# An edge loop on three engines: VectorE starts each tile at GpSimd's signal, one operand and three project steps moved

## The reference, cut to what matters

```python
def gatv2(x, src, dst, Ws, bs, Wd, bd, attn):
    H, D = attn.shape
    fs = (x @ Ws + bs).reshape(-1, H, D)
    fd = (x @ Wd + bd).reshape(-1, H, D)
    e = jax.nn.leaky_relu(fs[src] + fd[dst], 0.2)        # 10625 edges, gathered rows
    logits = jnp.einsum('ehd,hd->eh', e, attn)
    m = jax.ops.segment_max(logits, dst, num_segments=N)
    ex = jnp.exp(logits - m[dst])
    denom = jax.ops.segment_sum(ex, dst, num_segments=N)
    alpha = ex / denom[dst]
    out = jax.ops.segment_sum(alpha[:, :, None] * fs[src], dst, num_segments=N)
    return jax.nn.elu(out)

h = gatv2(x, src, dst, W1s, ...); h = layer_norm(h + x, ...)
out = layer_norm(gatv2(h, src, dst, Wos, ...), ...)      # the second graph attention
mix = mixer(xn)                                          # 12 heads, random features, then @ proj_w.T
x = x + out + mix; x = x + ffn(layer_norm(x))
```

## Time and profile before

| | |
|---|---|
| median of three runs | 1391.21 us (1389.6 to 1395.74) |
| the profiled execution | 1399.78 us, of it 1398.0 us span |
| loop 1, first lap's gather to last scatter | 105.56 to 434.26 us |
| loop 2, first lap's gather to last scatter | 652.52 to 999.53 us |
| busy share: PE, DVE, ACT, POOL | 76%, 66%, 40%, 44% |

### The profile page before, as it was taken

The page is one execution under the profiler, slowest core; times in us unless marked ns, Lnnn a source line. Parts: engine busy times, 40 slices in busy tenths (PEclk is TensorE's granted clock), DMA queues, the critical chain, the costliest instruction groups (busy, mean ns, idle before and its releaser), DMA issues.

```text
span 1398.0 us, 15907 instructions
## 1 busy us (share of the span) xinstructions
PE 1057.6 (76%) x5539; PEld 872.6 (62%) x5539; DVE 927.5 (66%) x1650; ACT 563.9 (40%) x736; POOL 616.7 (44%) x581
## 2 busy tenths in 40 slices
PE   5975655555542687898999999819587998999982
PEld 5963433333321687897787877617455997888871
DVE  6648777777774798544544454475358665999993
ACT  3304333333331898200434334420045324777760
POOL 1027777777773000014777777787400000333330
PEclk9988567778785789898799999958887899999995
DMA  9956666666766750257777776758423027999986
GB/s 335 354 193 174 197 199 196 195 198 196 203 197 169 174 163 1 79 144 232 227 218 220 198 214 191 257 161 246 103 77 118 6 102 279 396 399 406 399 329 176
DMA packets 85032, 290.84 MB, mean 208 GB/s; under 512 B 15970, under 2 KB 37768, under 8 KB 84341
## 3 DMA queue, kind: packets, MB, share of 16 engines
q0 software_dynamic: 34656, 145.11, 34.8%
q1 hardware_dynamic: 46822, 130.71, 27.7%
q10 hardware_dynamic: 3488, 14.16, 2.6%
HBM read 258.31 MB, written 31.62 MB: 207 GB/s over the span
## 4 chain that ended last, share of the span: by engine, by line
PE 37%; POOL 31%; issue 11%; DMA 9%; DVE 8%; ACT 3%; SPq 1%; DVEq 0%; POOLq 0%; ACTq 0%
POOL dense_logits L584 12%; PE ps L1461 10%; PE ps L1462 10%; PE ps L1463 10%; POOL ring_s L573 10%; POOL ring_d L579 9%; DMA ring_d<-table_dst,dst_i 4%; PE ps L1558 3%; PE ps L1542 1%; PE ps L1492 1%; DMA dl_b<-dense_logits 1%; DMA y_in<-y_rows 1%; DVE ring_s L1016 1%; DMA dl_a<-dense_logits 1%; ACT de L726 1%
## 5 line engine op out<-in xcount | busy, mean ns | idle before, releaser
L1016 DVE TENSOR_TENSOR ring_s<-ring_s,ring_d 128x776 f32<-128x776 f32 (+1 forms) x168 | 162.1, 965 | 244.1 <-DMA ring_d<-table_dst,dst_i 243.9
L573 POOL DMA_INDIRECT ring_s<-table_src,src_i x168 | 168.3, 1002 | 317.6 <-DVE fd_stage L945 257.8
L1521 PE MATMUL ps<-hot_s,hot_d 128*125 128x512 f16 (+1 forms) x840 | 185.5, 387 | 154.6 <-DVE hot_s L1023 154.5
L1521 PEld LDWEIGHTS ps<-hot_s,hot_d 128*125 128x125 f16 x840 | 116.1, 179 | 224.2 <-DVE hot_s L1023 165.0
L584 POOL DMA_INDIRECT dense_logits<-logits,cell_i x168 | 209.7, 1248 | 53.9 <-issue 50.0
L579 POOL DMA_INDIRECT ring_d<-table_dst,dst_i x168 | 168.9, 1005 | 76.7 <-issue 50.6
L700 ACT ACTIVATE hot_d<-iota_h,dst_bias 128x626 f16<-128x626 f16 x84 | 68.6, 816 | 217.5 <-PE ps L1521 217.5
L1461 PE MATMUL ps<-wp,at 128*125 128x384 f32 x300 | 107.3, 358 | 11.4 <-issue 4.4
L612 POOL COPY gather_i<-lst 128x1 int32 (+1 forms) x16 | 7.4, 462 | 237.7 <-DVE lst L1381 142.4
L1462 PE MATMUL ps<-wp,at 128*125 128x384 f32 x300 | 105.0, 350 | 0.0
L1463 PE MATMUL ps<-wp,at 128*125 128x384 f32 x300 | 104.8, 350 | 0.0
(11 more groups left out here) (252 smaller groups left out, 2338.9 us busy)
## 6 DMA issues: line engine op xcount, KB each, us to landing
eraw<-in_moe_w_dram SPq DMA_DIRECT2D x50, 768.0 KB, 6.7
raw<-in_moe_w_dram SPq DMA_DIRECT2D x44, 768.0 KB, 7.2
dense_logits<-neg ACTq DMA_DIRECT2D x1, 12288.0 KB, 43.6
mix_w<-in_qkv_wT_dram SPq DMA_DIRECT2D x18, 384.0 KB, 5.6
dl_a<-dense_logits SPq DMA_DIRECT2D x2, 2187.5 KB
dl_b<-dense_logits SPq DMA_DIRECT2D x2, 2187.5 KB
y_in<-y_rows SPq DMA_DIRECT2D x5, 672.0 KB
ring_s<-table_src,src_i POOLq DMA_INDIRECT x168, 4.1
```

The source lines that it names most:

```text
L573: pool.indirect_dma_start(out=ring_s[:, j, 0:WL[l]], out_offset=None, in_=table_src[l], in_offset=bass.IndirectOffsetOnAxis(ap=src_i[:, t: ...
L1016: dve.tensor_tensor(ring_s[:, j, 0:WL[l]], ring_s[:, j, 0:WL[l]], ring_d[:, j, 0:WL[l]], ALU.add).then_inc(z_ready[l], 1)
L1521: last = pe.matmul(ps[0:P, b, o:o + s1 - s0], hot_d[:, j, c * P:(c + 1) * P], hot_s[:, j, s0:s1], start=start and (n <= 5 or n == 9), stop ...
```

## The change

There are four edits.

1. **A signal and a wait.** Each lap of GpSimd that issues gathers raises `edge_turn[l]` by one, after its wait for `edge_done` and before the source gather (`pool.sem_inc`). In the program this makes one semaphore instruction a lap: it takes over the wait for `edge_done`, which was part of the gather's own instruction before. VectorE waits at tile t, for t from 3 to 81, until the signal of lap t - 3 has been given (`turn`).
2. **`total` moves to the front of a tile**, right behind the wait and ahead of `edge_sum`, in both loops.
3. **The attention row of loop 2 goes to PSUM.** `scale_attention(1)` writes it to `att_ps` in banks 6 and 7, and `weigh` reads it there. So the mixer may use six banks: `num` goes to bank 4 or 5 beside `kv`, at column `NUM_AT` = 130, and the transposes of the mixer's output use one pair of banks (4 and 5) instead of two, so that those of tile t wait for the low part of tile t - 1.
4. **`PROJ_FROM` becomes 67.** The last three project steps (17 to 19) then stand behind the last `total`.

```diff
-PROJ_FROM = ET - PROJ_STEPS
+PROJ_FROM = ET - PROJ_STEPS + 3
+TURN_LAG = 3
...
+        att_ps = ps[:, 6:8, :].rearrange("p a b -> p (a b)")[:, 1024 - D:1024]
...
-                b = (0 if n == 3 else 4) + 2 * (t % 2)
+                b = 2 * (t % 2) if n == 3 else 4
...
                     pool.wait_ge(edge_done[l], t + 1)
                     if t + G < ET:
+                        pool.sem_inc(edge_turn[l], 1)
                         gather_src(t + G)
                         gather_dst(t + G)
...
-                    last = act.copy(mix_out[:, :, 2 * r + h, :], ps[0:P, b, 0:T * (MD + 1)].rearrange(...))
+                    last = act.copy(mix_out[:, :, 2 * r + h, :], ps[0:P, b, NUM_AT:NUM_AT + T * (MD + 1)].rearrange(...))
...
-                dve.tensor_scalar(rows[:, 2, :], rows[:, 2, :], 0.8, None, ALU.mult).then_inc(att_scaled, 1)
+                dve.tensor_scalar((rows[:, 2, :], att_ps)[l], rows[:, 2, :], 0.8, None, ALU.mult).then_inc(att_scaled, 1)
+
+            def turn(l, t):
+
+                if TURN_LAG <= t < ET - G + TURN_LAG:
+                    dve.wait_ge(edge_turn[l], t - TURN_LAG + 1)
...
                 for t in range(ET):
+                    turn(0, t)
+                    if t >= 1:
+                        total(t - 1)
                     edge_sum(0, t)
                     if t + 1 < ET:
                         hot(t + 1)
                     weigh(t)
-                    if t >= 1:
-                        total(t - 1)
                     heads(t)
                 total(ET - 1)
...
-                    dve.scalar_tensor_tensor(out=ring_d[:, j, 0:D], in0=ring_s[:, j, 0:D], scalar=0.0, in1=rows[:, 2, :],
+                    dve.scalar_tensor_tensor(out=ring_d[:, j, 0:D], in0=ring_s[:, j, 0:D], scalar=0.0, in1=att_ps,
...
                 for t in range(ET):
-                    edge_sum(1, t)
+                    turn(1, t)
                     if t >= 1:
                         total(t - 1)
+                    edge_sum(1, t)
                     weigh(t)
...
-                back = (4, 1, 2, 2)[n]
+                back = (4, 1, 1, 2)[n]
...
+NUM_AT = 2 * (MD + 1)
...
-    if kind == "kv":
+    if kind in ("kv", "num"):
         return 4 + h
-    if kind == "num":
-        return 6 + h
```

More of the change, by code:

```diff
@@ L251, in build @@
         edge_done = [sem(f"edge_done{l}") for l in range(2)]
+        edge_turn = [sem(f"edge_turn{l}") for l in range(2)]
         scattered = [sem(f"scattered{w}") for w in range(W)]
@@ L813, in _ @@
                 else:
-                    last = act.copy(mix_out[:, :, 2 * r + h, :], ps[0:P, b, 0:T * (MD + 1)].rearrange("p (t d) -> p t d", t=T))
+                    last = act.copy(mix_out[:, :, 2 * r + h, :], ps[0:P, b, NUM_AT:NUM_AT + T * (MD + 1)].rearrange("p (t d) -> p t d", t=T))
                 last.then_inc(mix_used, 1)
@@ L1627, in _ @@
                         for f in range(2):
-                            last = pe.matmul(ps[0:P, b, t * (MD + 1):(t + 1) * (MD + 1)], mix_qp[:, h, f, t * P:(t + 1) * P],
+                            last = pe.matmul(ps[0:P, b, NUM_AT + t * (MD + 1):NUM_AT + (t + 1) * (MD + 1)], mix_qp[:, h, f, t * P:(t + 1) * P],
                                              mix_kv[:, h, f, :], start=f == 0, stop=f == 1)
```

## The result

| | before | after |
|---|---|---|
| median, same chip | 1397.37 us | 1389.61 us (1383.61 to 1396.2, 10 runs) |
| ratio | | 0.9957, 95% interval 0.9938 to 0.9976 |
| span of the profiled execution | 1398.0 us | 1388.3 us |

The change gains 6 us (3 to 9). I had forecast 32, and a time of 1359 us. The direction was right; the main step of the forecast was wrong. Single profiled executions lie several microseconds off their kernel's median, so times of steps read from profiles compare two kernels only that closely.

What follows compares the result with a forecast made beforehand. GpSimd's descriptor work was taken to bound loop 1, and loop 2 up to tile 64. Gains of 15 us (loop 1) and 17 us (end of loop 2) made 32, so 1391.2 - 32 = 1359 us; 8-in-10 range 1347 to 1400.

Steps and rivals of the forecast that it cites:

- the signal is given at least 0.76 us before the source gather starts: Loop 1: the running scatter covers the semaphore instruction's cost, and VectorE is held until near the scatter's start; 15 us gained.
- rival A: Both edge loops: the signal comes too early to hold VectorE, loop 1 gains 0, time 1379 us; chance 0.16.
- The arithmetic of the collision: GpSimd's jobs in the edge loops: one starting inside `edge_sum` is lengthened by the rest of `edge_sum` less 0.13 us.
- The free lap of 3.80 us: Edge loops: a GpSimd lap with nothing in its way takes 0.98, 0.97 and 0.94 us of work and three times 0.30.
- the 22 us: Loop 1: excess of scatter and gathers over their free durations, the most the edit can bring; 15 us of it taken.
- Rival B's locked case: Edge loops: `edge_sum` starts just before a GpSimd job every lap; with 0.6 us locked, 1435 us; rival's chance 0.22.
- whoever is first wins: Edge loops: VectorE's two-SBUF-operand instructions and GpSimd's descriptor work exclude each other at its start, the earlier one prevailing.
- Step 0 was to run at 904.4: Loop 2, first project step: reached at 901 with laps of 3.85 us, held by the mixer, 4.9 us earlier than before.
- 36 us for eight laps: Loop 2, step 0 to step 8's end: 35.1 plus a 3.8 us lap, less some 3 for `weigh` collisions; end at 940.5.
- Edit 4's overlap: End of loop 2: last `total` follows step 16's product, 14.5 us ahead of the last; dense stage begins 17 us earlier.
- Rival C: End of loop 2: logits loads go slower beside other traffic, that gain fails, 1370 us; chance 0.62 together with the main forecast.
- The mixer's end: Loop 2: the mixer runs at its own pace on TensorE and ScalarE, ends at 904.10 us; six banks cost nothing.

Runs made afterwards that it cites:

- e1: The changed kernel without the signal and without VectorE's wait for it: 1388.86 us, 0.9958 of the kernel before.
- e2: The changed kernel with a lag of 2 laps for 3, so the signal is asked for one lap later: 1389.63 us, 0.997 of before.
- e7: The changed kernel with the signal raised by a GpSimd memset of an unread column instead of a bare semaphore instruction: 1459.36 us, 1.0467 of before.
- e15: e11 with, in loop 2 too, an unread VectorE instruction of hot's kind and size between total and edge_sum: 1357.19 us, 0.9721 of before.
- e11: e7 with `hot` ahead of `edge_sum` in loop 1: 1404.8 us, 1.007 of the kernel before.
- e6: The kernel before with only the attention row of loop 2 in PSUM, six mixer banks and one transpose bank pair: 1391.3 us, 0.9987 of before.
- e8: The kernel before with only PROJ_FROM set to 67: 1393.21 us, 0.9992 of before.
- e10: e1 with project steps 0 to 9 three tiles earlier, steps 10 to 16 left in place: 1382.27 us, 0.9916 of before.
- e13: e7 with three one-column VectorE memsets ahead of `edge_sum` in every tile: 1464.94 us, 1.051 of before.

## Why the prediction was wrong

**The failed step** is "the signal is given at least 0.76 us before the source gather starts", read as 0.76 and little more, so that VectorE would be held near the scatter's start. What stands in the earlier trace rows gave only a lower bound: the semaphore instruction costs no gap. I filled the upper side with a choice. `total`, which had to wait for the signal, started 3.56 us ahead in the row above, and e1 and e2 show that the wait does nothing. This is rival A, to which I gave 0.16 with the words "nothing shows a depth over one"; nothing showed a depth of one either. The Trainium skill's "Perfetto Trace Analysis", section "Sequencer Loop", says that engine instructions are pushed into a queue and that a control instruction starts executing. With more than one descriptor job in that queue loop 1 gains 0, and the trace agrees: 434.84 against 434.26 us.

**What was right.** The arithmetic of the collision: a job that starts inside `edge_sum` pays the rest less 0.13 (e7, by calculation and row 1.73; over the more than 1400 such jobs of all runs the sum is off by 0.01 us in the mean). The free lap of 3.80 us (3.83 in e15), and the 22 us as the most to be had in loop 1 (e11's ends 19.0 us ahead of before's). Rival B's locked case: I wrote 1435 us with 0.6 us locked; e7 had 0.76 locked and took 1459. So too the weighing of the Trainium skill's "SBUF — State Buffer", section "Who interferes with whom": its remark that a probe showed `tensor_tensor` not stalling DMA, for which it infers a reason, does not hold here, by e7's 1.73 us.

**What was read wrongly.** The words "whoever is first wins" are too short even for the earlier trace rows, where `weigh` is first by 0.04 us and gives way: the first wins if it is 0.05 us ahead. And 1399.8 - 32 is 1367.8, not 1367.6; nothing else hangs on it.

**Mis-sized terms at the end of loop 2** (17 forecast, 7.9 measured, 9 missing). Step 0 was to run at 904.4, held by the mixer; with laps of 4.05 us instead of 3.85 it ran at 910.83, behind the mixer's end (890.1). From there to the end of step 8 I took 36 us for eight laps; it took 40.1. The first seven took 35.3, as before (35.1): the 3 us that I took off for `weigh` did not show. The eighth took 4.8 instead of 3.8. The two jobs under the weight halves ate 2 of these 3 us. Before:

```profile
924.13 2.16 POOL L573 DMA_INDIRECT ring_s<-table_src,src_i  x1 [0.30 <-issue]
...
928.57 2.19 POOL L584 DMA_INDIRECT dense_logits<-logits,cell_i  x1 [0.30 <-issue]
```

and after:

```profile
923.77 3.20 POOL L588 DMA_INDIRECT dense_logits<-logits,cell_i  x1 [0.30 <-issue]
...
929.08 3.14 POOL L583 DMA_INDIRECT ring_d<-table_dst,dst_i  x1 [0.30 <-issue]
```

Both now start 0.2 us into a half, and wait for nearly all of it. So step 8 ended 10.4 us behind the forecast. From there to the last product it took 53.2 us, as before (53.3), and so the last product and the last `total` were some 10.4 us behind too. The maxima followed in 3.6 us where I had taken 4.7, which gave 1.1 back. Edit 4's overlap itself was sized about right: the last `total` leads the last product by 14 us (14 forecast), and the maxima follow directly. Rival C, slower loads of the logits, is ruled out as a cause of the loss: no maximum waits for them. Rival A's time, 1379, was too early for the same reason: it had the products 1.2 us later than before, and they came 6.5 later.

**The sum.** 0 for 15 in loop 1 and 8 for 17 at the end: 8 us by the stations, 9.7 by the spans, 6 by the timed ratio. Of the 8, some 1.8 lie ahead of loop 2, whose first lap's gather starts at 650.73 (652.52 before) though loop 1 ended 0.6 later. No edit is aimed at that stretch, the start moves between 647.34 (e8) and 652.52 us in kernels whose loop 1 is that of before, and the timed ratio fits the smaller rest. How the 6 us divide among edits 2, 3 and 4 is not shown: edit 2 was not run alone, and the intervals of e6 and e8 leave room for up to 5 and 4 us. What the stations suggest is that edit 3 frees laps but leaves the last `total` behind the products (e6), and edit 4 frees the last `total` but puts step 0 later (e8); e10 shows that later step 0 to be worth another 6 us.

**The mixer's end** was taken as fixed at 904 us. It moves between 884 and 904 us in kernels with laps of 4.0 to 4.2 us, and TensorE's granted clock accounts for it. From 648 us to the mixer's end the mean granted share was 0.94 of 256 us in the profile of before and 0.93 of 255 in that of e6, against 0.99 of 242 in that of after and 0.99 of 238 in that of e8: time and share multiply to 236 to 241 us in all four. In before the granted share was 0.53 from 652 to 685 us, nearly all of it at the lower level (0.50, 1.2 GHz of 2.4); in e6 it was 0.50 from 880 us to the end of the mixer. TensorE was busy for 96% of both stretches or more; ahead of them it had been busy for 9.5 of 12 us in before and 19.9 of 20 us in e6. Why the clock fell there in these executions and not in the others stays open. The six banks cost the mixer nothing that these figures show.

## What to carry to other kernels

A bound from one side is not a position: before a wait is costed, ask of the row how early and how late its signal can come, and from what it is ordered. A bare semaphore instruction beside descriptor jobs did not say here when a job was due; to say when a job is done or due, hang the signal on an instruction that the engine executes, or on a landing. And when two engines exclude each other, synchronising them fixes the loss or the gain in every lap: check the start times to 0.05 us, and put an instruction that collides with nobody ahead of the one that does.

## What the runs showed of the hardware that I had not expected

- A bare semaphore instruction of GpSimd passed at least 3.87 us (loop 1, after) and at least 8.36 us (loop 1, e2) ahead of the gather that follows it in the text, in the laps where it led most.
- A GpSimd memset between descriptor jobs is free: 0.12 us and 0.19 of issue in the place of 0.30. VectorE's `total` starts 0.04 us behind its end.
- The exclusion is decided within some 0.04 us: `edge_sum` 0.05 us ahead of a gather costs the gather 0.79 us (e13); `weigh` 0.01 us ahead costs it nothing and is itself stretched from 0.95 to 1.00 us (e11).
- An operand in PSUM takes VectorE out of GpSimd's way: 326 descriptor jobs that began inside `weigh` with its row in PSUM took 0.94 to 0.99 us; with the row in SBUF one took 1.74.
- Three one-column memsets on VectorE delay what follows by 0.02 us (from 0.09 behind the start of `total` in e7 to 0.11 in e13), the 626-column TENSOR_SCALAR by 0.34 (to 0.43, e15).
